# A transformer block on one core: the layouts in which x, Wqkv and Wproj arrive

## What is computed

```python
qkv = einsum('btc,ec->bte', x, Wqkv) + bqkv
q = elu(q * scale) + 1;  k = elu(k * scale) + 1
kv = k * v
k_cumsum, kv_cumsum = cumsum(k, axis=1), cumsum(kv, axis=1)
denom = clip(sum over d of q * k_cumsum, EPS)
y = q * kv_cumsum / denom
x = layernorm(x + einsum('btc,ec->bte', y, Wproj) + bproj)
h = gelu(bq(x) @ bq(w_fc).T + b_fc)          # bq: blocks of 32 share an exponent
x = layernorm(x + bq(h) @ bq(w_proj).T + b_proj)
```

## Time and profile before

| | us |
|---|---|
| median of 3 runs | 276.52 (276.45 to 277.63) |
| profiled execution: span from first to last instruction | 273.3 |
| what lies around the span, by the median | 3.2 |
| busy in the span: TensorE / VectorE / ScalarE / GpSimd | 240.0 / 238.9 / 151.0 / 155.0 |
| copies of xT on ScalarE (16) | 9.3 |
| transposes of x on TensorE (64, overlapping) | 10.4 |

### The profile page before, as it was taken

One profiled execution on the slowest core, in us unless ns is written; L12 is line 12 of the kernel. 1 busy time (PEld: TensorE's weight loads), 2 busy tenths in 40 slices (PEclk: granted clock), 3 DMA queues, 4 the chain that ended last, 5 costly groups with the idle time before them and its releaser, 6 DMA issues.

```text
span 273.3 us, 3668 instructions
## 1 busy us (share of the span) xinstructions
PE 240.0 (88%) x1204; PEld 143.4 (52%) x1204; DVE 238.9 (87%) x513; ACT 151.0 (55%) x246; POOL 155.0 (57%) x118
## 2 busy tenths in 40 slices
PE   7999889997999899989999899989999989838761
PEld 7546636653566446644656356644664455524340
DVE  1398997998998999899989999899989997978962
ACT  2663277745556851855475754685285646332823
POOL 1076466575376656476566737675647656655851
PEclk9999999999999999999999999999999997979997
DMA  6940020036202473227304490238224530642022
GB/s 155 365 97 2 0 78 1 2 70 155 46 0 38 77 193 42 38 39 190 81 0 77 114 160 0 41 64 205 38 36 44 110 83 0 65 90 78 0 79 77
DMA packets 49474, 20.70 MB, mean 76 GB/s; under 512 B 38960, under 2 KB 49200, under 8 KB 49456
## 3 DMA queue, kind: packets, MB, share of 16 engines
q1 hardware_dynamic: 47824, 20.20, 32.7%
q10 hardware_dynamic: 1632, 0.27, 0.6%
HBM read 7.35 MB, written 4.19 MB: 42 GB/s over the span
## 4 chain that ended last, share of the span: by engine, by line
DVE 56%; PE 25%; DMA 8%; POOL 4%; issue 3%; ACT 2%; SPq 1%; ACTq 0%; POOLq 0%; DVEq 0%
DVE vbank L857 12%; PE abank L1116 8%; DVE hq L758 7%; DVE vbank L821 6%; PE dbank L1193 5%; DVE kvsum L799 4%; DMA h<-in_L_ffn_w_fc_dram 4%; POOL h_round L380 3%; PE hbank L1184 3%; DVE r L815 3%; DVE r L869 3%; DVE vbank L834 3%; DMA xqT<-xq 2%; DVE h_pow L750 2%; DVE kf L782 2%
## 5 line engine op out<-in xcount | busy, mean ns | idle before, releaser
L1116 PE MATMUL abank<-xT,WqkvT 128*128 128x512 f32 x176 | 81.6, 599 | 3.6 <-DVE kf L782 2.2
L380 POOL TENSOR_TENSOR h_round<-h,h_inv 128x1024 f16<-128x1024 f32 x32 | 66.5, 2079 | 31.2 <-DVE h_inv L753 28.5
L527 ACT ACTIVATE h<-hbank 128x512 f32<-128x512 f32 x64 | 36.7, 595 | 51.3 <-PE hbank L1184 51.0
L1116 PEld LDWEIGHTS abank<-xT,WqkvT 128*128 128x128 f32 x176 | 31.1, 190 | 36.2 <-issue 23.7
L857 DVE TENSOR_REDUCE vbank<-h 128x32 f32<-128x1024 f32 x32 | 39.1, 1221 | 1.6 <-ACT h L527 1.5
L349 POOL TENSOR_TENSOR qk<-qf,ksum 128x512 f32<-128x512 f32 x16 | 23.5, 1469 | 29.4 <-DVE ksum L794 18.6
L1184 PE MATMUL hbank<-w_fcT,xqT 128*128 128x512 bf16 x128 | 39.1, 387 | 0.0
L521 ACT ACTIVATE expz<-abank,zbias_neg 128x512 f32<-128x512 f32 x30 | 20.6, 687 | 31.9 <-PE abank L1116 31.4
L1193 PE MATMUL dbank<-w_prT,hT 128*128 128x256 bf16 x256 | 34.4, 279 | 1.9 <-DMA hT<-hq 1.3
L1148 PE MATMUL bbank<-WprojT,y 128*128 128x256 f32 x128 | 32.0, 380 | 0.0
L1193 PEld LDWEIGHTS dbank<-w_prT,hT 128*128 128x128 bf16 x256 | 25.2, 100 | 9.5 <-issue 3.3
(11 more groups left out here) (102 smaller groups left out, 357.4 us busy)
## 6 DMA issues: line engine op xcount, KB each, us to landing
x_sb<-in_L_attn_x_dram SPq DMA_DIRECT2D x8, 512.0 KB, 3.9
out_dram<-o_sb SPq DMA_DIRECT2D x7, 512.0 KB, 3.5
h<-in_L_ffn_w_fc_dram SPq DMA_DIRECT2D x1, 1024.0 KB, 9.6
h<-in_L_ffn_w_proj_dram SPq DMA_DIRECT2D x1, 1024.0 KB, 11.1
Wqkv_sb<-in_L_attn_Wqkv_dram SPq DMA_DIRECT2D x3, 256.0 KB, 6.3
out_dram<-o_sb SPq DMA_DIRECT2D x4, 128.0 KB, 1.7
hT<-hq SPq DMA_TRANSPOSE x28, 3.1
Wproj_sb<-in_L_attn_Wproj_dram ACTq DMA_DIRECT2D x1, 256.0 KB, 7.2
```

The source lines that it names most:

```text
L380: nc.gpsimd.tensor_tensor(h_round[:, t % 2].rearrange("p (g j) -> p g j", j=BLOCK_K), h[:, t].rearrange("p (g j) -> p g j", j=BLOCK_K), h_ ...
L527: nc.scalar.activation(h[:, t, half * HALF:(half + 1) * HALF], hbank[half][:, :], ACT.Gelu).then_inc(s_h, 1)
L1116: last = nc.tensor.matmul(ps[:, :], WqkvT[:, k, e * P:(e + 1) * P], xT[:, k], start=(k == 0), stop=(k == CC - 1))
```

## The change

The host hands over x also transposed (2, 256, 2048), and Wqkv and Wproj only transposed. TensorE's transposes of them and ScalarE's copies go, and with them Wqkv_sb, Wproj_sb and four semaphores. xT has two buffers, one for each parity of the chunk, filled by transfers of 512 KB (512 tokens, 2 KB, to a run). x_sb is still loaded, for the residual. The scaling of Wq and Wk moves to VectorE, in place, ahead of zbias. In VectorE's list `split_biases` and `w_exponents(0)` move behind features of chunk 0. Some waits that stood before `transpose_x` now stand before projections.

```diff
-            sp.dma_start(x_sb[:, 0], x_d[0, 0]).then_inc(s_x[0], 16)
-            sp.dma_start(Wqkv_sb[:, 2:4], Wqkv_d[:, 2:4]).then_inc(s_wk, 16)
-            sp.dma_start(Wqkv_sb[:, 0:2], Wqkv_d[:, 0:2]).then_inc(s_wq_in, 16)
-            sp.dma_start(Wqkv_sb[:, 4:6], Wqkv_d[:, 4:6]).then_inc(s_wv, 16)
+            sp.dma_start(WqkvT[:, :, C:2 * C], wqkv_d[:, :, C:2 * C]).then_inc(s_wk, 16)
+            sp.dma_start(xT[:, 0], xt_d[0, 0]).then_inc(s_xT[0], 16)
+            sp.dma_start(WqkvT[:, :, 0:C], wqkv_d[:, :, 0:C]).then_inc(s_wq_in, 16)
+            sp.dma_start(WqkvT[:, :, 2 * C:], wqkv_d[:, :, 2 * C:]).then_inc(s_wv, 16)
             sp.dma_start(w_fc_sb, w_fc.rearrange("(e p) c -> p e c", p=P)).then_inc(s_wfc, 16)
+            sp.dma_start(xT[:, 1], xt_d[1, 0]).then_inc(s_xT[1], 16)
+            sp.dma_start(x_sb[:, 0], x_d[0, 0]).then_inc(s_x[0], 16)
             sp.dma_start(w_pr_sb, w_pr.rearrange("(e p) c -> p e c", p=P)).then_inc(s_wpr, 16)
             sp.dma_start(x_sb[:, 1], x_d[1, 0]).then_inc(s_x[1], 16)
...
+            def load_xT(n):
+                wait(sp, s_qkv[2], 2 * n - 2)
+                sp.dma_start(xT[:, n % 2], xt_d[n % 2, n // 2]).then_inc(s_xT[n % 2], 16)
...
             load_bias_rows()
+            load_xT(2)
             load(2)
+            load_xT(3)
             turn_hq(0, 0)
...
             def step(s):
                 n = s + 1
                 turn_xq(n)
+                n = s + 4
+                load_xT(n)
+                n = s + 1
                 turn_hq(n, 0)
...
             load_table()
-            copy_xT(0, 0, abank[0])
-            copy_wqkT(0, hbank[0])
-            copy_xT(0, 1, abank[1])
-            copy_wqkT(1, hbank[1])
-            copy_wprojT()
             activate(0, 1, 0, abank[0])
-            copy_wvT()
             activate(0, 0, 0, hbank[0])
...
+            def scale_wqk(part):
+
+                lo = (C, 0)[part]
+                dve.wait_ge((s_wk, s_wq_in)[part], 16)
+                nc.vector.tensor_scalar(WqkvT[:, :, lo:lo + C], WqkvT[:, :, lo:lo + C], scale_sb[:, 0:1], None, ALU.mult).then_inc(s_wT, 1)
+
             dve.wait_ge(s_scale, 16)
+            scale_wqk(0)
+            scale_wqk(1)
             dve.wait_ge(s_bqkv, 16)
...
+            feature(0, 1, 0, abank[0])
             split_biases()
-            w_exponents(0)
-            feature(0, 1, 0, abank[0])
             sum_k(0, 0, 0)
             feature(0, 0, 0, hbank[0])
             feature(0, 1, 1, abank[1])
+            w_exponents(0)
             sum_k(0, 0, 1)
...
             def project(n, a, c, ps):
 
-                if isinstance(n, int) and n == 0:
-                    pe.wait_ge(s_wT, (2, 1, 3)[a])
-                wait(pe, s_xT, 2 * n + 2)
+                if n == 0 and a == 2:
+                    pe.wait_ge(s_wv, 16)
+                elif n == 0:
+                    pe.wait_ge(s_wT, 2 - a)
+                wait(pe, s_xT[n % 2], 8 * (n - n % 2) + 16)
...
-            transpose_x(0, 0, 0, abank[0])
-            transpose_wqk(0, hbank[0])
-            transpose_x(0, 0, 1, abank[1])
-            transpose_wqk(1, hbank[1])
             project(0, 1, 0, abank[0])
-            transpose_wproj()
-            transpose_wv()
-            pe.wait_ge(s_wT, 2)
             project(0, 0, 0, hbank[0])
             project(0, 1, 1, abank[1])
             project(0, 0, 1, hbank[1])
             project(0, 2, 0, bbank[1])
-            pe.wait_ge(s_f[1], 1)
-            transpose_x(1, 1, 0, abank[0])
             project(0, 2, 1, dbank)
             pe.wait_ge(s_f[1], 2)
-            transpose_x(1, 1, 1, abank[1])
+            project(1, 1, 0, abank[0])
             denominators(0)
-            project(1, 1, 0, abank[0])
             transpose_rec(0, 0)
```

More of the change, by code:

```diff
@@ L50, in wait, with block_kernel @@
     engine.wait_ge(sem, value)
-def block_kernel(nc, x, Wqkv, bqkv, Wproj, bproj, scale, w_fc, b_fc, w_pr, b_pr, out):
+def block_kernel(nc, x, xt, wqkv_t, bqkv, wproj_t, bproj, scale, w_fc, b_fc, w_pr, b_pr, out):
     BATCH, T, C = x.shape
@@ L1085, in _ @@
                 nc.tensor.transpose(dbank[:, 0:P], ident[:, :], ident[:, :])
-            def transpose_wqk(part, ps):
-                pe.wait_ge((s_wk, s_wq_in)[part], 16)
-                for c in range(CC):
-                    for e in range(2):
-                        last = nc.tensor.transpose(ps[:, c * C + e * P:c * C + (e + 1) * P],
-                                                   Wqkv_sb[:, (2, 0)[part] + e, c * P:(c + 1) * P], ident[:, :])
-                last.then_inc(s_wT_ps, 1)
-            def transpose_wv():
-                pe.wait_ge(s_wv, 16)
-                for c in range(CC):
-                    for e in range(2):
-                        last = nc.tensor.transpose(bbank[0][:, c * C + e * P:c * C + (e + 1) * P],
-                                                   Wqkv_sb[:, 4 + e, c * P:(c + 1) * P], ident[:, :])
-                last.then_inc(s_wT_ps, 1)
-            def transpose_x(n, b, c, ps):
-                wait(pe, s_x[b], 8 * (n - b) + 16)
-                for t in range(TILES):
-                    last = nc.tensor.transpose(ps[:, t * P:(t + 1) * P], x_sb[:, b, t, c * P:(c + 1) * P], ident[:, :])
-                last.then_inc(s_xT_ps, 1)
-            def project(n, a, c, ps):
-                if isinstance(n, int) and n == 0:
-                    pe.wait_ge(s_wT, (2, 1, 3)[a])
-                wait(pe, s_xT, 2 * n + 2)
+            def project(n, a, c, ps):
+                if n == 0 and a == 2:
[3 more added lines that the diff above has]
+                wait(pe, s_xT[n % 2], 8 * (n - n % 2) + 16)
                 e = CC * a + c
                 for k in range(CC):
-                    last = nc.tensor.matmul(ps[:, :], WqkvT[:, k, e * P:(e + 1) * P], xT[:, k], start=(k == 0), stop=(k == CC - 1))
+                    last = nc.tensor.matmul(ps[:, :], WqkvT[:, k, e * P:(e + 1) * P], xT[:, n % 2, k], start=(k == 0), stop=(k == CC - 1))
                 last.then_inc(s_qkv[a], 1)
@@ L1194, in down @@
                 last.then_inc(s_down, 1)
-            def transpose_wproj():
-                pe.wait_ge(s_wproj, 16)
-                for c in range(CC):
-                    for e in range(CC):
-                        last = nc.tensor.transpose(bbank[1][:, c * C + e * P:c * C + (e + 1) * P], Wproj_sb[:, e, c * P:(c + 1) * P], ident[:, :])
-                last.then_inc(s_wproj_ps, 1)
             def transpose_w_fc(c):
@@ L1288, in step @@
                 n = s + 2
+                wait(pe, s_kv, 2 * n)
                 project(n, 0, 0, abank[1])
@@ L1305, in step @@
                 project(n, 2, 1, abank[1])
-                n = s + 3
-                wait(pe, s_f[0], 2 * n)
-                transpose_x(n, n % 2, 0, abank[0])
                 n = s
@@ L1311, in step @@
                 down(n, 3)
-                n = s + 3
-                wait(pe, s_kv, 2 * n)
-                transpose_x(n, n % 2, 1, abank[1])
                 n = s + 1
@@ L1343, in step @@
                 n = s + 3
+                wait(pe, s_f[0], 2 * n)
                 project(n, 1, 0, abank[0])
@@ L1470 @@
     from concourse.bass_utils import run_bass_kernel_spmd as _run
+    inputs = dict(inputs)
+    inputs['xT'] = _np.asarray(inputs['L0_attn_x']).transpose(0, 2, 1)
+    inputs['WqkvT'] = _np.asarray(inputs['L0_attn_Wqkv']).T
+    inputs['WprojT'] = _np.asarray(inputs['L0_attn_Wproj']).T
     nc = _bacc.Bacc("TRN2", target_bir_lowering=False, num_devices=1)
```

64 lines of the change are left out of this document (14 added, 50 removed).

## The result

The changed kernel took 283.94 us (median of four runs, 281.79 to 284.60) against 276.82 us of the kernel before beside it: a ratio of 1.0229, with an interval of 1.0183 to 1.0275. The profiled execution took 284.0 us, of which the span is 282.1, so 1.9 us lie around it.

The account below looks back on a forecast made before the run. VectorE's own work was taken to set the pace of a step. Span 273.3 + 5.4 (start) - 0.1 + 0.7 (clock fall) = 279.3 us, plus 3.2 around it: 282.5, range 278.4 to 285.5.

Parts of the forecast that it names:

- the likeliest case: The forecast itself: the changed kernel is slower at 282.5 us, own range 280.5 to 284.0, chance 0.42.
- the steady part: Chunks after the start: removed transposes and copies cost 0, 0.1 us off at chunk 1, one more clock fall 0.7.
- what surrounds the span: Time outside the profiled span: 3.2 us, by which the profiled execution lay under the median of 276.52.
- The late weights: At the start, the moved weights' exponents come 2.5 us later, then GpSimd's rounding and products; denominators start 2.8 us late.
- The exclusion of VectorE and GpSimd: At the start, GpSimd's product beside VectorE's quantise takes 2.16 us, not 1.27; by the skill's rule, total 0.9 less.
- The clock at the start: TensorE idles at least 4.7 us before the denominators and drops to half clock; second residual 5.4 us late in all.
- The sign of being wrong that I had named: Steady steps shorter than 29.4 us, which would mean that TensorE or ScalarE had set them.
- A clock that holds: Rival: weights late at the start but TensorE's clock stays full, only 2.6 us lost; 279.0 us, chance 0.20.
- Cold first projections: Rival: TensorE idles until 7.2, first projections run at half clock, kf 1.6 us later; 284.1 us, chance 0.18.
- Faster by an early start of VectorE: Rival: VectorE begins chunk 0 at 10.8 and keeps 1.7 us if rounding begins by 16.1; 274.7 us, chance 0.08.
- falls in every step: Rival: TensorE's clock falls in every steady step, 3.5 us in place of 0.7; 285.3 us, chance 0.05.

## Why the prediction was right, and where it was not

It named 282.5 us (278.4 to 285.5) and slower; 283.94 was measured, inside the range and, by 0.06 us, in the likeliest case. The mechanism at the start was right; that the number is so near is partly luck. In the profiled execution the start cost 5.6 us (I had 5.4), the steady part gave back 0.8 (I had a cost of 0.6), the tail cost 4.0 (I had nothing), and what surrounds the span was 1.3 us less than I took. So a missing term of 4.0 us is set off by two errors of 1.3 to 1.4 us the other way. By its steps:

**The late weights.** Right in mechanism and almost in each time. The first kf was at 11.62 for 10.8, the exponents at 15.70 for 15.0, the rounding at 18.69 for 18.0, the end of the products at 25.74 for 25.0, the denominators at 25.88 for 25.1. One error runs through all: I had Wq landing at 8.2 and it landed at 9.25, and all else waited for zbias behind its scaling. The scaling itself, for which I took 0.7 us from a row out of PSUM, took 0.49. The late landing belongs to this execution: in the five other profiled executions that scale Wq at this place its scaling began at 8.26 to 8.80 us, and the first kf of the three with this order was at 10.58 to 10.95 us, around my 10.8. The first 768 KB were there by 6.46 us, ahead of my 7.2. Why the landing varies the traces don't say. The two runs on the order show the cause: 1.0011 with it undone, 1.0253 with it alone.

**The exclusion of VectorE and GpSimd.** My sum stretched one product of GpSimd to 2.16 us. The rule of the Trainium skill (SBUF — State Buffer, "Who interferes with whom"), by which whoever issued first goes first, would have made it 0.9 us less, I wrote, since GpSimd would be first. The trace agrees with the rule and not with my use of it. The first product issued at 22.27, VectorE's hq at 22.49; it was hq that was stretched, to 2.12 us, and then the second product, issued at 23.49 while hq ran, took 2.25. The two took 3.47 us together, my 3.43. Here the alternation cost each side once, and being first helped GpSimd for one instruction only.

**The clock at the start.** Right: the pause of 5.47 us ended in 0.50, the denominators took 3.55 us (I had 3.4) and the transposes of the reciprocals 1.97 (1.96). Too much was the 0.75 us for output projections at half speed: the clock was back at 34.3 us, as they began, not at 35. (My bound of 5.5 us for this came from the start of the kernel, where I inferred half clock from transposes of 1.11 us in place of 0.60; the granted clock reads 1.00 there.) That error and the 0.7 us by which everything was late cancel, and the second residual is at 38.36 where I had 38.2. The agreement there is better than the reasoning.

**The steady part.** I took the removed work at 0 and one more fall at 0.7. The sign of being wrong that I had named, steps under 29.4 us, came true: the two steps of the changed kernel without a fall took 29.35 and 29.32 us. So VectorE's own work does not set the pace alone, and the change is worth 0.3 to 0.4 us per step. My reading made nothing of the small waits that the page had. Over the four steps from `residual_2` of 75.01 us VectorE's waits come to 3.5 us in the kernel before, 2.5 of them for GpSimd's h_round, and to 2.9 us with the steps filled, 2.0 of them for h_round. That is 0.6 of the 1.5 us gained; the traces don't show where the rest comes from, nor which part of the change it belongs to. The falls were priced rightly and counted rightly by accident: two, at 112 and 143 us, each behind the pause for xqT that I had named, at 0.6 to 0.7 us each, while the one of the kernel before at 226 us did not come. That makes one more, but not, as I wrote, in steps that all look like the last.

**The tail.** The step that was missing. I had "from there on the order and the durations are those of today", although showed a pause of 4.37 us in the tail and half clock behind it: a stretch whose length had no reason to stay the same. In the changed kernel the pause is 4.83 us and the clock came back 10 us later than before, for 2.6 us of span; a second fall behind the pause of 2.02 us cost the other 1.3. The run with the filled tail has neither fall and loses nothing there. Why the first stayed half for some 14 us in this execution, 10 in the run with the steps filled, 7 in the run with the start filled and 3.4 in the kernel before is open, as is why the pause of 2.02 us is followed by a fall in some executions only; the work behind the pause is the same, with small pauses of 0.52 us between the down projections in all of them.

**What lies around the span.** The mis-sized term on the other side: 3.2 us, the median less the span of one execution. Within one and the same execution it is 2.1 to 2.3 us for the old layouts and 1.9 to 2.0 for the new. The rest was that the profiled execution was a good one. With 1.9 my sum would have been 281.2; the error in this term stood in for a third of the missing tail.

**The rivals.** A clock that holds gave 279.0 by my sum: the run with the start filled had the denominators' row 2.7 us late (I had 2.8 for the denominators) and 280.4 us, with other falls left. Cold first projections: the first took 2.22 us in place of 1.88, and nobody noticed, since zbias came later still. Faster by an early start of VectorE: its condition was a rounding by 16.1, and it came at 18.69. The reordered start, in which the products don't wait for the rounding, shows that an early start can be kept: 1.5 us ahead at the second residual. The range did not fit its own account: I said that it leaves out falls in every step, and at 285.3 us it holds them.

## What to carry to other kernels

Work taken from an engine that has room can cost time, if it was what kept TensorE's clock up (here two falls of 0.6 to 0.7 us, against 0.3 to 0.4 us gained per step): look for the pauses that the removal leaves, and hold the longest pauses already there against the clock behind them. Where a load comes earlier, follow what each list puts behind it; here three features, a sum and the splits put ahead of a maximum, and a rounding that GpSimd does ahead of two urgent products, cost 3.6 us at the start (5.6 us late, and 2.0 with the order undone), more than the change gained in all its steps. And compare a span with the runs' mean clock beside it before anything is read from its distance to the median.

## What the runs showed of the hardware that I had not expected

Matmuls that nobody reads took 1.0 to 1.7% off the kernels' time where they were placed in pauses of 4.4 to 5.5 us (ratios 0.9897 for 1, and 1.0057 and 1.0089 for 1.0229); in the pauses of 1 us their gain shows in the traces alone. The clock fell in or behind pauses of 0.93 us (at 110.8), 1.55, 1.98, 4.83 and 5.47 us, and held through others of 0.95 and 1.41 us (at 99.25 and 70.12 in the changed kernel); behind the pause of 2.02 us of the tail it did both, in different executions. So a pause alone does not decide; the trace does not say what else does. Half clock cost about the same factor, 1.8 to 1.9, whatever the instruction: f32 output projections and denominators went from 1.03 to 1.91 us and from 1.92 to 3.55, and a bf16 down projection from 1.04 to 1.91. And the same program, the kernel before, run again, spread over 275 to 281.5 us with its mean clock from 0.982 down to 0.954.
